# A two-layer recurrent network on one core: unread products behind the chain of states, the feed-forward bias by GpSimd, and other slice tables

## The reference

```python
# layer 0, attention: 16 heads, d_k = 8, d_v = 64, causal softmax, output projection
# layer 0, mixture of experts: layer norm, top-2 of 8 experts, capacity 512, silu-gated
x1 = x + attention(norm(x)) * silu(moe(norm(x)))
# layer 1, attention: gated delta rule, 4 heads of 32, chunks of 32 tokens
for chunk in chunks:                      # 16 chunks: the chain of states
    u_new = u - w @ S
    o = q @ S + tril(q @ k.T) @ u_new
    S = S + k.T @ u_new
out1 = rms_norm(mix(o, ema(v))) @ Wo
# layer 1, feed-forward: two transformer layers with a local window of 64, 8 heads of 64
for l in range(2):
    y = y + local_attention(shift(y)) @ wo[l]
    h = layer_norm(shift(y)) @ w1[l] + b1[l]
    a, g = split(h)
    y = y + (a * gelu(g)) @ w2[l] + b2[l]
final = x1 + silu(y) * out1
```

## Time and profile before

| | us |
|---|---|
| median of 3 runs (lowest, highest) | 2554.92 (2554.34, 2555.77) |
| profiled execution | 2570.71 |
| its span, first to last instruction | 2568.6 |
| granted TensorE clock, mean | 0.858 of full speed |

### The profile page before, as it was taken

The page is one execution under the profiler, slowest core; times in us unless marked ns, Lnnn a source line. Parts: engine busy times, 40 slices in busy tenths (PEclk is TensorE's granted clock), DMA queues, the critical chain, the costliest instruction groups (busy, mean ns, idle before and its releaser), DMA issues.

```text
span 2568.6 us, 51135 instructions
## 1 busy us (share of the span) xinstructions
PE 2057.2 (80%) x20756; PEld 1172.1 (46%) x20756; DVE 1351.8 (53%) x3137; ACT 1389.1 (54%) x3603; POOL 530.4 (21%) x597
## 2 busy tenths in 40 slices
PE   4597678977797878978797868978798868977677
PEld 3143434454445634555344634555344634554434
DVE  6424474555647374555646364554637465555352
ACT  1644357653867267653767257653767257653343
POOL 2712040302212040302212040301303040301130
PEclk9698579988899789987898779997899878997877
DMA  9124500020001100020101110020100210000000
GB/s 284 54 82 145 132 19 3 1 51 10 10 2 31 21 17 3 1 51 10 10 2 21 32 17 3 1 51 10 9 2 12 41 17 3 1 14 6 1 1 5
DMA packets 129737, 75.93 MB, mean 30 GB/s; under 512 B 76067, under 2 KB 121468, under 8 KB 127454
## 3 DMA queue, kind: packets, MB, share of 16 engines
q1 hardware_dynamic: 125406, 66.34, 10.5%
q0 software_dynamic: 4096, 6.32, 2.0%
HBM read 41.55 MB, written 33.16 MB: 29 GB/s over the span
## 4 chain that ended last, share of the span: by engine, by line
PE 40%; DVE 17%; ACT 15%; issue 9%; POOL 8%; DMA 1%; POOLq 0%; DVEq 0%; SPq 0%; ACTq 0%
PE PS L1406 4%; POOL area_b L1712 4%; PE PS L1269 4%; ACT work_a L786 3%; PE PS L1419 3%; PE PS L585 3%; ACT area_b L1503 3%; POOL area_b L1720 2%; PE PS L1377 2%; PE PS L1304 2%; ACT work_a L803 2%; DVE work_a L913 2%; DVE area_b L1599 2%; PE PS L741 2%; PE PS L1339 2%
## 5 line engine op out<-in xcount | busy, mean ns | idle before, releaser
L1712 POOL TENSOR_TENSOR area_b<-area_b,tables 128x256 f32<-128x256 f32 x256 | 212.9, 851 | 830.7 <-DVE area_b L1599 830.7
L786 ACT ACTIVATE work_a<-PS,work_a 128x512 bf16<-128x512 f32 (+3 forms) x512 | 264.8, 536 | 78.8 <-DVE work_a L913 77.8
L913 DVE TENSOR_REDUCE work_a<-PS 128x2 f32<-128x1024 f32 (+3 forms) x256 | 200.7, 820 | 109.7 <-PE PS L537 109.5
L1503 ACT ACTIVATE area_b<-PS,neg_max 128x192 f32<-128x192 f32 (+1 forms) x512 | 202.2, 417 | 99.3 <-DVE neg_max L1639 76.0
L803 ACT ACTIVATE work_a<-PS 128x1024 f32<-128x1024 f32 (+1 forms) x192 | 169.4, 882 | 136.4 <-PE PS L567 135.8
L1269 PE MATMUL PS<-wqkv,area_b 128*128 128x512 f32 x384 | 200.4, 654 | 11.5 <-DVE area_b L1599 10.2
L1304 PE MATMUL PS<-area_b 64*128 64x192 f32 (+1 forms) x1024 | 158.0, 444 | 64.4 <-ACT shiftT L1489 37.0
L1726 POOL TENSOR_TENSOR rstd_b<-var_eps_b,minus_half 128x4 f32<-128x4 f32 x16 | 16.4, 1025 | 808.3 <-DVE var_eps_b L123 808.3
L585 PE MATMUL PS<-work_a 128*64 128x512 f32 (+3 forms) x1024 | 179.3, 453 | 0.0
L1304 PEld LDWEIGHTS PS<-area_b 64*128 64x128 f32 x1024 | 106.1, 256 | 116.2 <-ACT shiftT L1489 41.5
L1519 ACT ACTIVATE area_b<-PS 128x768 f32<-128x768 f32 (+1 forms) x128 | 97.4, 761 | 103.7 <-PE PS L1347 102.7
(11 more groups left out here) (319 smaller groups left out, 4209.0 us busy)
## 6 DMA issues: line engine op xcount, KB each, us to landing
work_a<-stack_d SPq DMA_DIRECT2D x32, 512.0 KB, 9.2
stack_d<-area_b SPq DMA_DIRECT2D x48, 192.0 KB, 3.1
stack_d<-area_b SPq DMA_DIRECT2D x32, 128.0 KB, 2.7
area_b<-in_L_attn_x_dram SPq DMA_DIRECT2D x4, 512.0 KB, 5.5
slots_in<-work_a SPq DMA_DIRECT2D x8, 256.0 KB, 4.3
stack_d<-work_a SPq DMA_DIRECT2D x4, 512.0 KB, 7.3
work_a<-xnT_d SPq DMA_DIRECT2D x8, 256.0 KB, 3.9
work_a<-in_L_attn_x_dram SPq DMA_DIRECT2D x8, 256.0 KB, 3.0
```

The costliest lines, as they stand in the source:

```text
L786: nc.scalar.activation(dump0[:, n % 2 * T:n % 2 * T + (i + 1) * P], PS[:, a:a + (i + 1) * P], ACT.Exp, bias=neg_max0[:, k:k + 1], accum_ou ...
L913: nc.vector.reduce_max(neg_max0[:, 2 * g * NT + i:(2 * g + 2) * NT:NT], at[:, :, Q_AT[i]:Q_AT[i] + (i + 1) * P], AX_X, negate=True).then_i ...
L1503: nc.scalar.activation(dump2[:, n % 4 * 256:n % 4 * 256 + w], PS[:, a:a + w], ACT.Exp, bias=neg_max2[:, k:k + 1], accum_out=sums2[:, k:k + ...
L1712: nc.gpsimd.tensor_tensor(to[:, n, :, r, :], src[:, n, :, 1 - r, :], table(2 * n + 1, t)[:, 32 * r:32 * r + 32].unsqueeze(1).to_broadcast( ...
```

## The change

Three things are changed.

1. Behind the chain of states TensorE issues seven bf16 products of 128 x 128 by 128 x 512 into bank 5. Nobody reads them and nothing is signalled.
2. The bias leaves TensorE. `b2_sb` holds the bias in all 128 partitions (loaded by a broadcast DMA), GpSimd adds it to `y` right behind `rstd_b`, and VectorE waits for that ahead of its last addition. The new waits of GpSimd are for the two readers of `y` (`low`, `step_mm`).
3. All ten tables are other ones.

```diff
+            FILL = 7
...
             last.then_inc(sd["out_mm"], 1)
+            for _ in range(FILL):
+                nc.tensor.matmul(bank(5), ident16[:, :], causal16[:, :].unsqueeze(1).to_broadcast([P, NT, P]),
+                                 start=True, stop=True)
             yield
...
                     o = bank(6, t * P, (t + 1) * P)
-                    if c == 0:
-                        nc.tensor.matmul(o, ones_row, b2_sb[:, l * P:(l + 1) * P], start=(t == 0),
-                                         stop=(t == 0), skip_group_check=True)
                     k = (l * 3 + c) * P
                     last = nc.tensor.matmul(o, glu[0:n, c * T + t * P:c * T + (t + 1) * P],
-                                            w2_sb[0:n, k:k + P], start=False, stop=True, skip_group_check=True)
+                                            w2_sb[0:n, k:k + P], start=(c == 0 and t == 0), stop=True,
+                                            skip_group_check=True)
...
             dve.wait_ge(s["w2_mm"], past("w2_mm", 1))
+            dve.wait_ge(s["biased"], past("biased", 1))
             nc.vector.tensor_tensor(y[:, :], y[:, :], bank(6), ALU.add).then_inc(s["y_out"], 1)
...
             nc.gpsimd.tensor_tensor(rstd_b[:, :], var_eps_b[:, :], minus_half[:, 0:NT], ALU.pow).then_inc(s["rstd"], 1)
+            gp.wait_ge(s["low"], past("low", 1))
+            gp.wait_ge(s["step_mm"], past("step_mm", 1))
+            nc.gpsimd.tensor_tensor(y[:, :].rearrange("p (t f) -> p t f", f=P), y[:, :].rearrange("p (t f) -> p t f", f=P),
+                                    b2_sb[:, l * P:(l + 1) * P].unsqueeze(1).to_broadcast([P, NT, P]), ALU.add
+                                    ).then_inc(s["biased"], 1)
```

More of the change, by code:

```diff
@@ L210, in network @@
         b1_sb = sb("b1_sb", DEPTH * 6)
-        b2_sb = sb("b2_sb", DEPTH * P, F32, 1)
+        b2_sb = sb("b2_sb", DEPTH * P)
         ln_sb = sb("ln_sb", 2 * DEPTH)
@@ L1690, in local_pool @@
             s, past, once = sb_, counted(PER_LAYER, b * DEPTH + l, HEAD_ENDS), counted(PER_BATCH, b, HEAD_ENDS)
+            y = ys[b % 2]
             def halves(buf, t):
@@ new lines, in network @@
+            "scalar": (0, 0, 0, 0, 0, 0, 0, 0, 0, 0, 0, 0, 6, 36, 42, 42, 44, 44, 44, 44, 44, 44,
+                44, 44, 44, 44, 44, 44, 47, 47, 47, 47, 47, 47, 47, 49, 49, 51, 52, 54, 55, 66, 71, 71,
+                85),
+            "vector": (0, 0, 0, 0, 0, 0, 0, 0, 0, 0, 0, 0, 25, 39, 41, 41, 41, 41, 41, 41, 41, 41,
+                41, 41, 41, 41, 41, 41, 45, 45, 46, 46, 46, 46, 47, 49, 50, 50, 50, 55, 56, 64, 69, 70,
+                76),
+            "gpsimd": (0, 0, 0, 0, 0, 0, 0, 0, 0, 0, 0, 0, 2, 3, 8, 9, 14, 15, 15, 15, 15, 15,
+                15, 15, 15, 15, 15, 15, 23, 24, 24, 28, 38, 40, 43, 46, 46, 46, 46, 46, 54, 58, 66, 72,
+                79),
@@ L2234, in network @@
+            "sync": (0, 0, 0, 0, 0, 0, 0, 0, 0, 0, 0, 1, 22, 41, 41, 41, 41, 41, 41, 41, 41, 42,
+                42, 42, 42, 42, 42, 42, 46, 46, 46, 48, 48, 48, 55, 59, 59, 59, 60, 60, 63, 63, 79, 79,
+                90),
         }
         A_AHEAD_OF_B = {
-            "tensor": (93, 93, 94, 94, 94, 94, 95, 96, 96, 100, 101, 101, 102, 102, 104, 106, 107, 107, 109, 110, 112, 113,
-                115, 116, 118, 119, 120, 122, 123, 129, 132, 133, 133, 133, 135, 138, 140, 144, 145, 145, 147, 147, 149, 149,
-                150, 151, 152, 154, 154, 157, 158, 158, 160, 164, 165, 165, 165, 165, 165, 165, 165, 165, 165, 166, 167, 167,
-                168, 169),
@@ new lines, in network @@
+            "scalar": (85, 88, 88, 91, 91, 94, 94, 95, 96, 99, 100, 100, 101, 101, 102, 104, 105, 107, 108, 110, 111, 112,
+                114, 116, 118, 119, 119, 121, 123, 129, 130, 130, 130, 134, 134, 138, 139, 141, 142, 144, 145, 148, 148, 150,
+                150, 152, 152, 156, 157, 157, 157, 157, 157, 158, 158, 158, 159, 160, 160, 163, 164, 165, 166, 167, 168, 170,
+                177, 178),
+            "vector": (93, 93, 93, 94, 94, 94, 94, 95, 96, 99, 100, 100, 101, 101, 102, 104, 105, 107, 108, 114, 115, 119,
+                119, 119, 119, 119, 120, 122, 125, 125, 126, 129, 129, 129, 134, 138, 139, 143, 143, 144, 144, 147, 148, 149,
+                150, 151, 152, 155, 157, 157, 158, 158, 159, 161, 163, 163, 164, 164, 164, 165, 165, 165, 166, 169, 169, 169,
+                169, 169),
@@ new lines, in network @@
+            "gpsimd": (86, 87, 87, 87, 87, 88, 88, 88, 88, 88, 91, 91, 91, 91, 94, 94, 94, 94, 96, 96, 98, 98,
+                101, 101, 101, 101, 101, 101, 103, 103, 106, 112, 115, 115, 115, 116, 120, 120, 120, 120, 122, 124, 124, 125,
+                125, 125, 126, 130, 133, 136, 136, 136, 136, 137, 137, 137, 137, 137, 137, 137, 152, 155, 165, 169, 169, 172,
+                175, 176),
+            "sync": (100, 100, 103, 103, 106, 108, 108, 110, 111, 113, 114, 115, 119, 119, 119, 119, 119, 124, 124, 124, 127, 128,
+                129, 129, 129, 129, 129, 129, 129, 130, 130, 130, 130, 138, 139, 144, 150, 152, 152, 152, 162, 164, 166, 171,
+                172, 172, 177, 180, 181, 181, 181, 181, 183, 183, 183, 184, 186, 186, 186, 187, 192, 192, 192, 192, 192, 192,
+                192, 192),
```

41 lines of the change are left out of this document (9 added, 32 removed).

## The result

The changed kernel took 2551.23 us (median of 20 runs, 2540.52 to 2558.72). The kernel before, run beside it, took 2558.32 (20 runs, 2551.29 to 2569.35). The ratio is 0.997, with a 95% interval of 0.9957 to 0.9983. It is faster by 0.3%, some 7 us, where 34 were forecast.

What follows compares the result with a forecast made beforehand. The prediction took TensorE, busy 80% of the span and often at half clock, as the bound. Terms -37 - 13 + 12 + 0 + 4 = -34 us took the median 2555 to 2521 us, range 2490 to 2558.

Steps and rivals of the forecast that it cites:

- bias products gone: TensorE's w2 in 16 layers: without 64 bias products each pair saves 0.58 us; -37 us, bounds -20 and -40.
- unread products: Behind the chain of states: seven products fill TensorE's idle time and the clock rises earlier; -13 us, bounds 0 and -15.
- addition by GpSimd: At each layer's normalization: the addition holds up VectorE's L126 by 0.75 us a layer; +12 us.
- tables, stretches and head: New order of work in all queues: 0 from the first B on, and +4 us in the head.
- The tables in the stretches: Queues from the first B on: no work added, no idle time to fill; 0, bounds -2 and +6 us per sequence.
- a stall of 1 us: Second layer: glu0 waits for mn and h2 for glu0, 1 us, offset by vanishing stalls of step and transposes.
- The bound of +6 for each of eight: Upper bound in us on the second layer's stall per sequence, with glu0 behind mn and step.
- The head: Work before B(0): +4 us, bounds -3 and +8; B(0) at 333 + 4, the forecast wrong if later than 341.
- The remainders inside the inverse: Head, VectorE: H42 and H43 stand ahead of the inverse's last steps and push its DMA round trip back 6 us.
- The experts: Head: they start behind unit 12, up to 4.4 us earlier; taken as -2 us.
- the faster rival: w2: the clock stays up without one-row products, a further -15 us, giving 2506; chance of faster than the sum 0.14.
- The slower rival: Second layer's feed-forward: clock stays low through h0, h1, h2, w2; up to 8 us a sequence, 2585; chance of slower 0.15.

Runs made afterwards that it cites:

- e7: The kernel before with no feed-forward bias at all, neither bias products nor addition, and no unread products; ratio 0.9865.
- e3: The kernel before with the seven unread products alone, tables of before; 2547.88 us, ratio 0.996.
- e17: As e20, but the feed-forward bias is not added at all: no product, no addition; ratio 0.9782 to the kernel before.
- e20: Same program as e1, measured a third time, on the chip of e19; ratio 0.9871 to the kernel before.
- e1: The changed kernel with all ten tables of before, so both edits with old tables; 2524.55 us, ratio 0.9867 to the kernel before.
- e4: The kernel before with the bias added by GpSimd alone, no unread products, tables of before; 2545.89 us, ratio 0.9948.
- e19: As e1, with new stretch-table entries 55 to 67 (second layer's end), but TensorE's 55 to 61 old; ratio 0.9925 to the kernel before.
- e5: Both edits with the old head tables and the new stretch tables; ratio 0.998 to the kernel before.
- e15: As e1, with the last 34 entries of each stretch table (a sequence's second layer) new; ratio 0.9974 to the kernel before.
- e8: Both edits with the new head tables and the old stretch tables; ratio 0.9929 to the kernel before.
- e10: As e1, but VectorE's head-table entries for H42 and H43 put them inside the first inverse; ratio 0.9905 to the kernel before.
- e14: As e1, with the first 34 entries of each stretch table (a sequence's first layer) new; ratio 0.9893 to the kernel before.
- e16: Same program as e1, measured again on another chip; ratio 0.9878 to the kernel before.
- e18: As e8, but SyncE's head table puts twelve stores of stack_d behind the store and load of low_d; ratio 0.9946 to the kernel before.
- e21: As e1, with stretch-table entries 34 to 54 (second layer's projections and attention) new; ratio 0.99 to the kernel before.
- e2: The kernel before with the ten new tables and neither edit; 2591.93 us, ratio 1.0139.
- e9: As e1, but GpSimd's addition waits until VectorE has done its four L126; ratio 0.9892 to the kernel before.
- e22: Both edits with old tables, but the bias is an 86th row of w2's third chunk, without GpSimd's addition; 2574.48 us, ratio 0.9825 to the kernel before.

## Why the prediction was wrong

The sign was right, the size was not: 7 us of 34. The step that failed is that of the tables, which the sum puts at 0 in the stretches and +4 in the head; they cost 26 us. By its own terms:

| term | forecast | measured |
|---|---|---|
| bias products gone | -37 | -35 (e7: 1.35% of 2626) |
| unread products | -13 | -10 (e3) |
| addition by GpSimd | +12 | +23 (e17 against e20) |
| tables, stretches and head | +4 | +26 (after against e1) |

The measured terms add up to +4. The 11 us to the measured -7 are what the two edits bring together beyond one by one (e1 against e3 and e4).

- **Bias products: right.** Their price of 0.58 us a pair holds. In e7 w2 alone became 54 us shorter (49.2 us for all 16 against 103.7), since it now also runs at the full clock in nearly every layer; some 20 of these do not show in the time. Of e7's gain the stretches have up to 4.3 us each (284.2 against 288.5, on different chips and from the long execution of before).
- **Unread products: right in size, rougher in mechanism.** Seven took 3.17 us, inside the 3.6 that were worked out, but L1229 still has 0.55 us of idle time before it where less than 0.3 was forecast. The clock was to rise 1 to 2 us after L1229's start. It did better than that or not at all: by its start in 3 of 8 sequences, and 3.6 to 4.8 us later in the others, as before. Which it is hangs on what else is changed (6 of 8 in e1, 1 of 8 in e3), so the term is 10 us alone and some 20 beside the other edit with the old tables. The forecast's smooth 1.6 us for each of eight was a mean of two cases.
- **The addition: mis-sized.** The step took the slowdown of L126 as its whole cost. That term was near, 0.88 for 0.75 us, but the kernel lost as much again elsewhere. The forecast's claim that `updated` between step and transposes would cover most of it did not hold: TensorE's wait ahead of the second layer's transposes is 1.71 us in the kernel after and in e19, as in e20, where 0.78 was the wait before. The Trainium skill, page "SBUF — State Buffer", section "Who interferes with whom", has a tensor_scalar of VectorE in a two-port mode contend with GpSimd for one port pair, and the one that issues second blocks until the other is done. The trace comes near it: four L126 took 2.05 us beside an addition of 1.26 that began just before them, where they take 1.11 alone, so they lost 0.94 of 1.26.
- **The tables in the stretches: the step that failed.** "No work is added, and nothing is idle there to be filled, so 0", and a stall of 1 us set against stalls that vanish. The stalls did come out even: 0.78 us of idle time went ahead of the step and 0.86 came ahead of `uw`, and from wo to pu TensorE is idle for 2.5 to 2.7 us in both orders. What the sum put at nothing is the clock on the unchanged work. From wo to pu the edits with the old order have 9.3 to 9.8 us at the lower clock, with the new order 13.7 to 14.6, as before the change; that is 1.7 us a stretch, 10 to 12 us in all. Over a whole stretch it is 72 to 76 us at the lower clock with the new end of the second layer (after, e5, e15, e19), 61 to 67 with the old second layer (e1, e8, e10, e14, e16, e18, e20) and 70 in e21. The bound of +6 for each of eight held the measured 2 to 3 us. That the mean stretch was forecast at 285 to 286 us and came out at 285.4 is luck: the edits with the old tables have 283.2 (e1).
- **The head: failed by a term that was left out.** B(0) started at 351.3 where 337 was forecast and 341 was named as a sign of being wrong. The remainders inside the inverse were priced at 6 us; they lengthened it by 5.5. The twelve stores ahead of `low_d`, another 6 us, are in SyncE's order, and the forecast looked at SyncE only from the first B on. The experts, which were to save 2 us by starting earlier, started at 148.2 after and at 147.2 before.
- **The rivals.** The clock stayed up through w2 as the faster rival said, but its -15 does not show in the time. The slower rival, low clock in the feed-forward part of the second layer, is what happened in the stretches, at 1.7 us a sequence instead of up to 8. It had other products slow: w2 kept the full clock (2.9 us), the hidden products changed by less than 0.5 us, and it was `uw` that took 3.1 us more and `updated` 1.5 us less. Its price was also added up wrongly: 12 times 2.85/8, 1.9 and a stall of 6 us give 12 us a sequence and not 8.

## What to carry to other kernels

When an order changes and no work is added, the waits are not all that can change. Here TensorE's idle time stayed the same and the same products took 1.8 us longer, so compare busy time and granted clock of the same work in both orders before calling an order free. Look at the DMA queues too: a store that another engine needs stood 6 us behind twelve others, and moving those twelve held up whoever waited for them (e18). Measure an edit and its new order apart, since here the edits were worth 1.3% and the order took 1.0% of it back. A bias on the contraction side can be a further row of a product that is there anyway, and then costs neither a product nor an addition.

## What the runs showed of the hardware that was not expected

- w2's products took 280 ns with 85, 86 and 128 rows alike. A bias product with one row and a full one behind it took 0.83 us, the full one alone 0.25.
- Over the 160 sequences of the 20 profiles the clock's rise comes in two places: from 1.9 us before to 0.2 us behind the start of L1229, or 2.9 to 6.2 us behind it, and nowhere between. Without the unread products it is always the later place (before, e2, e4, e7).
- The same products in another order, with the same idle time, were at the lower clock for 13.7 to 14.6 us a stretch instead of 9.3 to 9.8.
- GpSimd's addition was not slowed by VectorE beside it (1.26 us, and 1.27 alone in e9); VectorE bore the whole conflict.
- The same queues on one core gave stretches that differ by up to 7.6 us (279.2 to 286.8 in e22), each with its own places where the clock falls and rises; e1, e16 and e20, one program on three chips, differ by up to 2.5 us in the mean stretch (283.2 to 285.7).
